# Attention on one Trainium2 core: projections, output product and the turning of the shift row issued as two tiles of 64 columns

## The reference, cut to what matters

```
q = (x @ Wq), k = (x @ Wk), v = (x @ Wv)       # 2048 x 1024 each: 16 heads of 64
scores  = einsum("bhqd,bhkd->bhqk", q * s, k * s)   # s = 64 ** -0.25
weights = softmax(scores, axis=-1)             # float32
out = einsum("bhqk,bhkd->bhqd", weights, v)    # heads side by side: 2048 x 1024
return out @ Wo                                # Wo: 1024 x 128
```

## Time and profile before

| | |
|---|---|
| median of 3 runs | 3724.13 us (3724.11 to 3726.1) |
| profiled execution, its own time | 3729.04 us |
| its span | 3726.8 us |
| mean granted clock of TensorE | 0.952 |
| busy share: PE, DVE, ACT, POOL | 90%, 64%, 46%, 74% |

### The profile page before, as it was taken

One profiled execution on the slowest core, in us unless ns is written; L12 is line 12 of the kernel. 1 busy time (PEld: TensorE's weight loads), 2 busy tenths in 40 slices (PEclk: granted clock), 3 DMA queues, 4 the chain that ended last, 5 costly groups with the idle time before them and its releaser, 6 DMA issues. The chain is left out here.

```text
span 3726.8 us, 50341 instructions
## 1 busy us (share of the span) xinstructions
PE 3364.4 (90%) x19063; PEld 1785.5 (48%) x19065; DVE 2402.4 (64%) x3711; ACT 1716.2 (46%) x2081; POOL 2753.3 (74%) x1152
## 2 busy tenths in 40 slices
PE   5775688389999999999999499999999999998898
PEld 2222233245555555555555255555555555553798
DVE  5898699766666666666664466666666666663554
ACT  3331432145455555555555245555555555554454
POOL 1783187148888888888889278888888888898233
PEclk9898798789999999999999799999999999999899
DMA  1330233110000000000000100000000000000000
GB/s 25 133 115 29 64 118 107 28 28 1 4 1 4 2 3 4 1 4 1 2 1 1 40 3 1 4 4 1 4 1 4 1 4 2 1 1 12 26 18 15
DMA packets 61404, 76.19 MB, mean 20 GB/s; under 512 B 7274, under 2 KB 48820, under 8 KB 61108
## 3 DMA queue, kind: packets, MB, share of 16 engines
q1 hardware_dynamic: 59362, 72.71, 6.1%
q10 hardware_dynamic: 1810, 0.37, 0.1%
HBM read 66.24 MB, written 6.82 MB: 20 GB/s over the span
## 5 line engine op out<-in xcount | busy, mean ns | idle before, releaser
L1384 POOL TENSOR_TENSOR den_g<-den_g,p 128x1024 f32<-128x1024 f32 x896 | 2130.4, 2378 | 275.9 <-ACT p L1351 159.7
L1436 DVE TENSOR_REDUCE quarters<-psum 128x1 f32<-128x512 f32 x1960 | 1263.1, 686 | 780.2 <-PE psum L995 728.4
L1351 ACT ACTIVATE p<-psum 128x1024 f32<-128x1024 f32 x1024 | 1024.3, 1026 | 500.9 <-PE psum L1245 468.6
L1258 PE MATMUL psum<-p,v 128*64 128x512 f32 x4096 | 932.2, 597 | 0.0
L1258 PEld LDWEIGHTS psum<-p,v 128*64 128x64 f32 x4096 | 276.7, 137 | 611.9 <-issue 474.7
L995 PE MATMUL psum<-k_main,q_main 64*128 64x512 f32 x2048 | 437.4, 422 | 13.7 <-DVE quarters L1002 11.2
L1245 PE MATMUL psum<-q_main,k_main 64*128 64x512 f32 x2048 | 435.1, 421 | 7.1 <-PEq L1132 4.9
L1245 PE MATMUL psum<-q_rest,k_main 64*128 64x512 f32 x2048 | 406.4, 392 | 0.0
L1245 PE MATMUL psum<-q_main,k_rest 64*128 64x512 f32 x2048 | 406.0, 392 | 0.0
L1245 PE MATMUL psum<-row_shift,row_ones 64*128 64x512 f32 x2048 | 404.9, 390 | 0.0
L736 POOL TENSOR_TENSOR seen<-state,c_sb 128x2048 f32<-128x2048 f32 x64 | 285.2, 4458 | 72.0 <-DVE state L683 63.2
(11 more groups left out here) (259 smaller groups left out, 3281.1 us busy)
## 6 DMA issues: line engine op xcount, KB each, us to landing
c_sb<-bc_rows SPq DMA_DIRECT2D x64, 512.0 KB, 3.5
work<-bc_rows SPq DMA_DIRECT2D x32, 512.0 KB, 4.9
resid<-in_resid SPq DMA_DIRECT2D x8, 256.0 KB, 3.7
x_mid<-resid SPq DMA_DIRECT2D x8, 256.0 KB, 2.6
xa<-x_mid SPq DMA_DIRECT2D x8, 256.0 KB, 3.6
x_tok<-x_mid SPq DMA_DIRECT2D x8, 256.0 KB, 3.8
x_mid<-x_tok SPq DMA_DIRECT2D x8, 256.0 KB, 2.7
x<-x_mid SPq DMA_DIRECT2D x8, 256.0 KB, 2.8
```

The costliest lines, as they stand in the source:

```text
L1258: last = nc.tensor.matmul(o_bank[hi(h), :], vv[:, kt, hi(h)], p[:, u % LIVE, h, :], start=(kt == 0), stop=(kt == KT - 1))
L1351: nc.scalar.activation(flat(p[:, u % LIVE]), s_bank(u), ACT.Exp, scale=float(DH) ** -0.5).then_inc(p_ready, 1)
L1384: nc.gpsimd.tensor_tensor(sums, first, src, ALU.add).then_inc(added_g, 1)
L1436: nc.vector.reduce_max(quarters[:, to % 2, h, n:n + 1], bank_of["max", u, h], X_AXIS).then_inc(max_read, 1)
```

## The change

`turn_shift`, `project` and the output product issue each of their matmuls as two, for columns 0 to 63 and 64 to 127 of the weights, with the results on partitions 0 to 63 and 64 to 127, as `values` and the denominators' sums do. For the shift row the tile grows from 2 to 64 columns of weights for each of its 8 places; columns 2 to 63 hold zeros, written once by GpSimd at the start of phase 2. The tile is now shared by `attention_first` and `attention_pairs`. Its eight matmuls are issued with the two heads of a place next to each other instead of four of one head and then four of the other. All other instructions keep their order.

```diff
+        shift = ph.sbuf("shift", [P, 2 * TPC, 64], BF16)
...
                     nc.gpsimd.memset(experts["down_b"][:], 0.0).then_inc(cleared, 1)
-                    pool.wait_ge(cleared, 1)
+                    nc.gpsimd.memset(shift[:], 0.0).then_inc(cleared, 1)
+                    pool.wait_ge(cleared, 2)
...
 def turn_shift(nc, dst, shift, ident_bf):
-    for h in range(2):
-        at = 64 * h
-        for j in range(TPC):
-            last = nc.tensor.matmul(dst[at:at + 2, j * P:(j + 1) * P], shift[:, h * TPC + j, :], ident_bf[:],
+    for j in range(TPC):
+        for h in range(2):
+            last = nc.tensor.matmul(dst[hi(h), j * P:(j + 1) * P], shift[:, h * TPC + j, :], ident_bf[:],
                                     start=True, stop=True)
...
 def project(nc, dst, w, xaT, i):
     if i < 2 * CHUNKS:
-        return nc.tensor.matmul(dst, w[:, 1 - i // CHUNKS, :], xaT[:, piece(c)], start=True, stop=True)
+        for h in range(2):
+            last = nc.tensor.matmul(dst[hi(h), :], w[:, 1 - i // CHUNKS, hi(h)], xaT[:, piece(c)], start=True, stop=True)
+        return last
     for j in range(TPC):
-        last = nc.tensor.matmul(dst[:, j * P:(j + 1) * P], xaT[:, (c * TPC + j) * P:(c * TPC + j + 1) * P], w[:, 2, :],
-                                start=True, stop=True)
+        for h in range(2):
+            at = (c * TPC + j) * P + 64 * h
+            last = nc.tensor.matmul(dst[hi(h), j * P:(j + 1) * P], xaT[:, at:at + 64], w[:, 2, :], start=True, stop=True)
     return last
...
-                        last = nc.tensor.matmul(bank, w_o[:, g // CHUNKS % 2, :], o_raw[:], start=True, stop=True)
+                        for h in range(2):
+                            last = nc.tensor.matmul(bank[hi(h), :], w_o[:, g // CHUNKS % 2, hi(h)], o_raw[:], start=True, stop=True)
```

More of the change, by code:

```diff
@@ L1041, in attention_first @@
 def attention_first(nc, b, m, experts):
-    xaT, w_qkv, w_o, v, k_main, k_rest, q_main, q_rest, row_shift, quarters, ident_bf, psum = (
-        m[k] for k in "xaT w_qkv w_o v k_main k_rest q_main q_rest row_shift quarters ident_bf psum".split())
+    xaT, w_qkv, w_o, v, k_main, k_rest, q_main, q_rest, row_shift, quarters, shift, ident_bf, psum = (
+        m[k] for k in "xaT w_qkv w_o v k_main k_rest q_main q_rest row_shift quarters shift ident_bf psum".split())
     with Phase(nc, f"_{b}") as su:
         maxima = su.sbuf("maxima0", [P, 2 * TPC])
-        shift = su.sbuf("shift0", [P, 2 * TPC, 2], BF16)
         (step, proj_psum, rounded, raw_ready, rest_done_v, rest_done_g, v_read, max_psum, max_read, shift_ready,
@@ L1139, in attention_pairs @@
         m[k] for k in "xaT attnT w_qkv w_o v k_main k_rest q_main q_rest ones ident_bf psum".split())
-    row_shift, row_ones, quarters = (m[k] for k in "row_shift row_ones quarters".split())
+    row_shift, row_ones, quarters, shift = (m[k] for k in "row_shift row_ones quarters shift".split())
     o_raw, den_g, rec = (m[k] for k in "o_raw den_g rec".split())
@@ L1178, in attention_pairs @@
         maxima = su.sbuf("maxima", [P, 2 * TPC])
-        shift = su.sbuf("shift", [P, 2 * TPC, 2], BF16)
         (weights, out_weight, step, max_psum, max_read, shift_ready, shift_read, s_psum, p_ready, pv_done, added_g,
```

## The result

| | before | changed |
|---|---|---|
| median | 3725.11 us (3724.11 to 3731.58, 4 runs) | 3674.93 us (3671.68 to 3679.08, 4 runs) |
| ratio, 95% interval | | 0.9864 (0.9851 to 0.9877) |
| span of the profiled execution | 3726.8 us | 3671.3 us |
| mean granted clock of TensorE | 0.952 | 0.954 |

The changed kernel is 50.2 us faster by the medians, 46 to 56 us by the interval. The forecast was 3672 us, 52.2 us faster.

The account below looks back on a forecast made before the run. TensorE, always busy in the long loop, was taken as the bound. Gains of 34.8 + 11.2 + 6.2 = 52.2 us, taken from 3724.1, gave a median of 3672 us, with a range from 3664 to 3700.

Parts of the forecast that it names:

- The bound: In the long loop TensorE, busy 399.97 of 400 us, sets the length by the distances between its starts.
- Projections and output product: Keys' and queries' projection and output product, before the values: 0.20 us less at each of 174 uses, 34.8 us.
- Rival D: Two tiles reading the same moving columns are not served side by side: slower, fully serial 158 us, 3882 us; 4%.
- Values' projection: Behind the values, 56 pieces: gap of 0.10 and bare load of 0.107 us go, 11.2 us gained.
- Rival A: Small tiles don't pair, the values' projection takes 16 steps: only 2.4 us gained, 3722 us; 4%.
- rival E: About 62 ns of sequencer time per matmul slows values' projection and shift row: 29.9 us gained, 3694 us; 3%.
- Shift row: Between the values and the next turn, 62 times: the gap ahead goes, 0.10 us each, 6.2 us gained.
- Nothing for the fills and for the first projections: GpSimd's added memset ends before VectorE's work, costing nothing; `attention_first` counted as nothing, 0.9 us kept for the range's lower end.
- Late next: GpSimd is next: a group loses 0.90 us and takes 39.5; GpSimd keeps 1.9 of 2.8 us idle.
- rival B: Half the freed time returns as waits of a chain not running through TensorE: 3698 us; 6%.
- The shift's readiness: `make_shift` must finish before the turning, now about 0.30 us earlier; with its longest last step 0.34 us are left.
- Rival C: The 0.10 us gap belongs to waits, not shape; only bare loads shrink: 12 us gained, 3712 us; 3%.

Follow-up runs that it names:

- `after_again`: The changed kernel, unaltered, run once more on the same chip as the run beside it: 3671.95 us, ratio 0.9853 to the kernel before.
- `extra_128`: The changed kernel plus one tiny bf16 128*128 matmul, behind all waits, at 236 uses before the values: 3699.8 us, ratio 0.9927 to the kernel before.
- `shift_32`: The changed kernel with 32 columns of weights for the shift row instead of 64: 3679.42 us, ratio 0.9882 to the kernel before.
- `shift_48`: The changed kernel with 48 columns of weights for the shift row instead of 64: 3673.27 us, ratio 0.9862 to the kernel before.
- `maxima_earlier`: The changed kernel with each turn's third maxima step issued one score step sooner (MAX_AT 10 instead of 11): 3659.25 us, ratio 0.9819 to the kernel before.

## Why the prediction was right, step by step

- **The bound.** Right. TensorE's distances set the loop. The control row (the sums' turn) did not move, and GpSimd, the next engine, kept idle time.
- **Projections and output product, 0.20 us at 174 places, 34.8 us.** 0.147 + 0.051 = 0.198, 34.5 us. The pair of tiles that stream the same `xaT` or `o_raw` starts together: four matmuls in 0.91 us, exactly the sums' row. Rival D, which no fp32 row had excluded, falls on the changed kernel's own trace.
- **Values' projection, 0.20 us at 56 places, 11.2 us.** 0.214, 12.0 us. A step of two matmuls and two loads of 64 columns takes (1.04 - 0.27) / 7 = 0.110 us, no longer than one matmul and one load of 128 columns. Rival A falls, and with it rival E: sixteen matmuls start within 0.77 us, where the Trainium skill's 62 ns for each (TensorE: Matmul & The Clock Gate, Part 1), a figure it gives for the case without the hardware decoder, would take 0.93 for the fifteen steps. The trace doesn't show that case.
- **Shift row, 0.10 us at 62 places, 6.2 us.** 0.104, 6.4 us. The load of 64 columns beside a matmul of 128 moving columns in bf16 costs next to nothing, as taken from the values' projection. But the prediction charged the wider load 0.054 us, which was read from fp32 loads. In bf16 the listed load grew by half of that, from 83 ns to 111 (mean of the 512 loads of line 1021). It had less to hide than assumed, so the error was on the safe side.
- **Nothing for the fills and for the first projections.** The added fill took 0.53 us beside VectorE's fills and ended before them; the first projection starts 22.35 us behind the writing of `down_b` (22.12 in `after_again`), 22.21 before. What the first projections gained can't be told from the rest of what differs outside the loops.
- **Late next, rival B.** The group lost 0.94 us (0.90 forecast), and in the steady run of the loop none of it came back as a wait.
- **The shift's readiness** ("That just holds") did not hold. The prediction left 0.34 us of room for VectorE's longest step, with the turning about 0.30 earlier, and had no term for the 0.15 us between that step's end and the turning's start. At three shift rows TensorE waited, 0.8 us in all. It was too rare to matter for the time, not ruled out as the prediction had it.
- **Rival C** (the gap belongs to the waits) was given 3% with one argument from the trace. `extra_128` shows directly that it is false, and so does `shift_32` beside `shift_48`.
- **One reading was loose:** the prediction put 0.3 us ahead of every use down to VectorE's reading. That changed nothing in the sum, since the entry is nearly the same on both sides, but only 0.07 of it was a wait, as `maxima_earlier` shows.
- **The number.** The sum of the parts, 52.2 us, was meant for the distances, and these gave 52.9. The medians differ by 50.2 (46 to 56), the profiled spans by 55.5. The 3 us between the forecast and the measured median are less than the spread of single executions, so that closeness is partly luck; the agreement term by term is not.

What stays open: how much of the 4.7 us outside the loops is the change and how much is spread between executions, and why the gap at a change of size is as long as it is.

## What to carry to other kernels

Where TensorE is always busy, look at the distances between starts where the form of its matmuls changes, not at its busy share. Give neighbours in the queue the same tile size: splitting a 128-column matmul into two tiles of 64 columns costs nothing when both run side by side, and padding 2 columns to 64 bought 0.10 us for 0.005. Then look at what the engine now reaches sooner: here a step of VectorE that had always been in time was late at three places. Use a place that already has the wanted form as the template for the price; here it gave every term within 0.02 us.

## What the runs showed of the hardware

- A change of the tile size costs about 0.10 us between matmuls (0.522 instead of 0.423 us from the last start to the next), in fp32 and into bf16, and bares the first load (0.05 us for 64 columns, 0.10 to 0.11 for 128 in fp32).
- 2 and 32 columns are another size than 64; 48 is the same as 64.
- Two 128*64 tiles that read the same moving columns in fp32 run side by side: four matmuls of 512 columns in 0.91 us, as many as in the sums' row, whose tiles read different ones. With 128 moving columns two loads and two matmuls fit into 0.110 us, as long as one load and one matmul of 128 columns took.
- A weight load of bf16 is listed at 83 ns for 2 columns, 96 for 32, 104 for 48 and 111 for 64; in fp32 it is 137 for 64 and 191 for 128.
- Eight matmuls issued as four of one tile and then four of the other already start in pairs before the change, four steps in 0.18 us; issuing them alternately brought 0.01 us.
